# Raw edge counts turned by DMA for the last six blocks of a graph layer, instead of on TensorE

## What is computed

```python
def _L0_gnn_ref(x, edge_index, W, b):
    ...
    h = jnp.einsum('nd,od->no', x, W) + b
    deg = jnp.zeros((num_nodes,), dtype=h.dtype).at[row].add(1.0)
    deg_inv_sqrt = deg ** (-0.5)
    norm = deg_inv_sqrt[row] * deg_inv_sqrt[col]
    msg = norm[:, None] * h[col]
    out = jax.ops.segment_sum(msg, row, num_segments=num_nodes)
    return out
...
edge_index = jnp.stack([src, dst])
x = x + _L0_gnn_ref(_layernorm(x, axis=-1), edge_index, L0_gnn_W, L0_gnn_b)
x = x + _L0_ffn_ref(_layernorm(x, axis=-1)[None], ...)[0]
```

## Time and profile before

| what | value |
|---|---|
| median of three runs | 646.37 us |
| the profiled execution | 647.8 us |
| its span, first to last instruction | 646.1 us |
| TensorE busy | 550.3 us, 85% |
| VectorE busy | 477.6 us, 74% |
| ScalarE busy | 239.8 us, 37% |
| GpSimd busy | 207.8 us, 32% |
| mean granted TensorE clock | 0.94 of full speed |
| instructions | 12534 |

### The profile page before, as it was taken

How to read it: one execution, slowest core, us unless ns; L and a number is a source line. 1 busy time by engine, 2 the same in 40 slices (tenths; PEclk the granted TensorE clock), 3 DMA queues, 4 the chain that set the end, 5 groups by cost and what they waited for, 6 DMA issues and landing times.

```text
span 646.1 us, 12534 instructions
## 1 busy us (share of the span) xinstructions
PE 550.3 (85%) x3720; PEld 303.7 (47%) x3721; DVE 477.6 (74%) x1293; ACT 239.8 (37%) x366; POOL 207.8 (32%) x200
## 2 busy tenths in 40 slices
PE   1598999999989999999495999999999999999300
PEld 0243455544444455555383565656565655565100
DVE  8998966976308588898877767776767677664297
ACT  4232333233217133434542344443434343411370
POOL 2740000000000126656646344445353535141231
PEclk9989999999979999999587999999999999999755
DMA  5595111111113624434655696969696969273979
GB/s 210 192 387 213 36 34 34 34 34 34 34 34 132 259 99 144 180 136 164 209 175 156 190 292 180 290 188 286 193 274 203 282 199 265 82 127 112 242 219 277
DMA packets 51691, 110.34 MB, mean 171 GB/s; under 512 B 25618, under 2 KB 26031, under 8 KB 51632
## 3 DMA queue, kind: packets, MB, share of 16 engines
q1 hardware_dynamic: 41552, 78.06, 34.2%
q0 software_dynamic: 8896, 27.38, 20.4%
q10 hardware_dynamic: 1184, 4.20, 1.9%
HBM read 71.75 MB, written 33.67 MB: 163 GB/s over the span
## 4 chain that ended last, share of the span: by engine, by line
PE 70%; DVE 21%; issue 3%; DMA 2%; ACT 2%; DVEq 1%; POOL 0%; ACTq 0%; POOLq 0%; SPq 0%
PE ps L1883 7%; PE ps L1766 6%; PE ps L1767 6%; PE ps L1884 6%; PE ps L1885 6%; PE ps L1862 5%; PE ps L1864 5%; PE ps L1863 5%; PE ps L1690 4%; PE ps L1844 4%; PE ps L1691 3%; PE ps L1692 3%; DVE wbufs L1162 3%; DVE wbufs L1161 2%; PE ps L1634 2%
## 5 line engine op out<-in xcount | busy, mean ns | idle before, releaser
L515 POOL TENSOR_TENSOR work<-work 128x1024 f16<-128x1024 f32 x9 | 19.2, 2128 | 213.5 <-ACT work L883 213.5
L608 POOL DMA_INDIRECT acc_rows<-work,ids_out x24 | 52.3, 2180 | 106.7 <-DVE work L1487 106.7
L1766 PE MATMUL ps<-wbufs,rows_and_counts 128*128 128x512 f16 x200 | 75.8, 379 | 0.5 <-DVE wbufs L1267 0.5
L1767 PE MATMUL ps<-wbufs,rows_and_counts 128*128 128x512 f16 x200 | 75.8, 379 | 0.0
L1862 PE MATMUL ps<-rows_and_counts,wbufs 128*128 128x336 f16 (+2 forms) x256 | 74.8, 298 | 0.8 <-DVE rows_and_counts L1425 0.8
L1883 PE MATMUL ps<-wbufs,rows_and_counts 128*128 x192 | 73.8, 384 | 1.8 <-issue 1.3
L1863 PE MATMUL ps<-rows_and_counts,wbufs 128*128 128x336 f16 (+2 forms) x256 | 74.9, 298 | 0.0
L1864 PE MATMUL ps<-rows_and_counts,wbufs 128*128 128x336 f16 (+2 forms) x256 | 74.8, 298 | 0.0
L1884 PE MATMUL ps<-wbufs,rows_and_counts 128*128 x192 | 73.7, 384 | 0.0
L1885 PE MATMUL ps<-wbufs,rows_and_counts 128*128 x192 | 73.5, 383 | 0.0
L1440 DVE SCALAR_TENSOR_TENSOR wbufs<-stage,wbufs 128x1024 f16<-128x1024 f32 x56 | 67.0, 1218 | 7.4 <-ACT wbufs L910 6.9
(11 more groups left out here) (305 smaller groups left out, 1087.5 us busy)
## 6 DMA issues: line engine op xcount, KB each, us to landing
stage<-wst_in SPq DMA_DIRECT2D x72, 512.0 KB, 6.0
acc_rows<-work SPq DMA_DIRECT2D x10, 512.0 KB
x_rows<-work SPq DMA_DIRECT2D x10, 512.0 KB
t<-x_in SPq DMA_DIRECT2D x1, 4096.0 KB, 14.5
wbufs<-b_in ACTq DMA_DIRECT2D x8, 512.0 KB
wbufs<-acc_rows SPq DMA_DIRECT2D x8, 512.0 KB, 6.7
t<-x_in SPq DMA_DIRECT2D x1, 3072.0 KB, 10.2
t<-x_in SPq DMA_DIRECT2D x1, 2048.0 KB, 8.0
```

The lines of the kernel that those rows point to most:

```text
L1766: mm(o, ct_hi[:, cs], hs[:, at:at + HALF], start=(m == 0), stop=False, skip_group_check=True)
L1767: mm(o, ct_hi[:, cs], hs[:, D + at:D + at + HALF], start=False, stop=False, skip_group_check=True)
```

## The change

The raw counts of blocks 4 to 9 are turned by a transposing DMA each, from `raw16` to `ct_hi`, on SP's queue. The products of `count_turn` and the copies of `count_hi` are left out for these blocks. Two semaphores, `ct_in[0]` and `ct_in[1]`, count the transfers of even and odd blocks. ScalarE waits for the transfer of block m - 2 before it writes the first raw strip of block m into the same buffer, and TensorE waits for all six ahead of the degree products. Blocks 0 to 3 are turned as before.

```diff
+COUNTS_BY_PE = 4
...
+        ct_in = [sem(f"ct_in{i}") for i in range(2)]
...
@@ block.sync
                 sp.wait_ge(xs_done, m + 1)
                 sp.wait_ge(lin_done, m - 1)
                 sp.dma_start_transpose(xt[:, at:at + 2 * D].rearrange("p (b k) -> p b k", k=P), xs).then_inc(xt_in, 16)
+                for n, blocks in enumerate(STEP_BLOCKS):
+                    if n == m - 1 and blocks[0] >= COUNTS_BY_PE:
+                        k = blocks[0]
+                        sp.wait_ge(raw_read, 4 * k + 4)
+                        sp.dma_start_transpose(ct_hi[:, k * NP:(k + 1) * NP].rearrange("p (h d) -> p h d", d=P),
+                                               raw16[k % 2]).then_inc(ct_in[k % 2], 16)
@@ block.scalar, raw_out
                     a.activation(raw32, strip, ACT.Copy).then_inc(raw32_done, 1)
+                if j == 0 and m >= COUNTS_BY_PE + 2:
+                    act.wait_ge(ct_in[m % 2], 16 * ((m - COUNTS_BY_PE) // 2))
                 a.activation(hi, strip, ACT.Copy).then_inc(raw_read, 1)

             def count_hi(m, groups):
+                if m >= COUNTS_BY_PE:
+                    return
@@ block.tensor
             def count_turn(m, groups):
+                if m >= COUNTS_BY_PE:
+                    return
...
                     pe.wait_ge(raw_lo_done, m + 1)
-                    pe.wait_ge(count_hi_read, NG * (m + 1))
+                    pe.wait_ge(count_hi_read, NG * min(m + 1, COUNTS_BY_PE))
...
             turn(NT - 1)
-            pe.wait_ge(count_hi_read, NG * NT)
+            pe.wait_ge(count_hi_read, NG * COUNTS_BY_PE)
+            for i in range(2):
+                pe.wait_ge(ct_in[i], 16 * (NT - COUNTS_BY_PE) // 2)
```

## The result

The changed kernel took 641.11 us (median of 6 runs, 640.08 to 643.28) beside 646.06 (645.47 to 646.76) for the kernel before, a ratio of 0.9923 [0.9908, 0.9939]: 4.95 us faster where 2.99 was forecast, and 0.4 us outside the range. The profiled execution took 641.27 us (span 639.6) against 647.8 (span 646.1). The one before is 1.7 us above the median of its kernel, so the spans differ by 6.5 us where the medians differ by 4.95.

The account below looks back on a forecast made before the run. TensorE was taken to bound most steps, VectorE steps 4 and 5. Savings of 1.68 + 0.11 + 1.20 = 2.99 us from 646.37 gave 643.4 us; 8-in-10 range 641.5 to 646.0.

Parts of the forecast that it names:

- Steps 3, 6 and 7: TensorE-bound steps turning blocks 4, 7 and 8: each saves 0.45 + 0.11 us, 1.68 us together.
- Steps 4 and 5: VectorE feeds the last window: only block 6's second part, behind that window, counts, 0.11 us; the other 1.01 us become waiting.
- Block 9: In the tail: 0.44 us for its first part, 0.76 us for the second with the wait for ScalarE's copy; 1.20 us.
- the tail's clock: TensorE's clock drops to half after the degree products, slowing dense products; change counted as 0, ends 2.1 gained, 1.2 lost.
- the gap of 1.25 us behind the degree products: TensorE's idle time in the tail, at the branch for large counts; left out of the sum.
- My end for the clock: Far end of the forecast's own range: the clock's fall misses the tail's dense products, 2.1 us more gained.
- Rival 1: VectorE does not bind in steps 4 and 5, so the whole sum comes through: 4.0 us, 642.4; chance 0.08.
- Rival 2: Only the tail counts; what steps 3, 6 and 7 give is taken back: 1.2 us left, 645.2; chance 0.15.
- Rivals 3 and 4: 3: clock falls in step 5, 648.4, chance 0.08; 4: block 9's transfer lands late, from 9.1 us on, chance 0.04.

Follow-up runs that it names:

- e3: Changed kernel with TensorE's ten products for each of blocks 4 to 9 kept at their old places, read by nobody; 645.46 us, ratio 0.9985.
- e6: Changed kernel with VectorE's statistics of row blocks 2 to 9 in four pairs instead of two fours; 641.66 us, ratio 0.9925.
- e9: Kernel before with 72 unneeded one-column products at TensorE's start; 646.90 us, ratio 1.0013.
- r1: Unchanged copy of the changed kernel, measured again; 644.54 us, ratio 0.9976 to the kernel before.
- e8: Changed kernel with 50 unneeded one-column products at TensorE's start; 644.13 us, ratio 0.9963.
- r2: Unchanged copy of the changed kernel, measured again in another group; 645.82 us, ratio 0.9972 to the kernel before.
- r3: Unchanged copy of the changed kernel, measured again in another group; 644.31 us, ratio 0.9949 to the kernel before.
- e13: Kernel before with statistics in pairs and degree products spread in the linear layer, all blocks turned by TensorE, no unneeded products; 639.77 us, ratio 0.9891.
- e12b: Second measurement of the changed kernel with statistics in pairs, degree products spread and fifty unneeded products at TensorE's start; 637.40 us, ratio 0.9859.
- e8b: Changed kernel with 50 unneeded one-column products at TensorE's start, measured in another group; 643.23 us, ratio 0.9936.
- e11: Changed kernel with statistics in pairs and degree products spread in the linear layer's quarters; 641.35 us, ratio 0.9895.
- e12: Changed kernel with statistics in pairs, degree products spread and fifty unneeded products at TensorE's start; 636.81 us, ratio 0.9836.
- e10: Changed kernel with the hundred degree products spread through the third and fourth quarter of row block 8's linear layer; 644.91 us, ratio 0.9967.

## Why the prediction was right and wrong

*Steps 3, 6 and 7, 1.68 us.* Right: 0.55 + 0.55 + 0.56 = 1.66 us in the first profile, and e3, which puts the products back, has 15.21 us again.

*Steps 4 and 5, 0.11 us.* The size was right (0.13), one reason only half. Step 5 is VectorE's: the five products that took 1.36 us in the earlier trace rows took 1.72,

```profile
133.70 1.72 PE L1646 MATMUL ps<-wbufs 128*128 128x320 f16 x5
```

and e6 takes the step to 15.05. In step 4 something else gave back what the products had left. The third window and what follows, after:

```profile
117.90 0.85 PE L1646 MATMUL ps<-wbufs 128*128 128x320 f16 x5
118.86 0.44 PE L1654 MATMUL ps<-wbufs 128*128 128x320 f16 x2
119.61 0.39 PE L1704 MATMUL ps<-wbufs 128*128 128x512 f16 x1
```

and before:

```profile
118.97 0.85 PE L1634 MATMUL ps<-wbufs 128*128 128x320 f16 x5
119.66 0.43 PE L1642 MATMUL ps<-wbufs 128*128 128x320 f16 x2
120.32 0.39 PE L1690 MATMUL ps<-wbufs 128*128 128x512 f16 x1
```

From the window's start to the next weight product it is 1.71 us now and was 1.35, although the two products of the turn stood in it then. What its two further pairs wait for was not tried.

*Block 9, 1.20 us.* Right by the timelines: the linear layer runs on from its second quarter into the degree products, and e9 against r1 gives 1.21 us. The transfers took 3.4 to 4.7 us where I expected 3 to 4.5, and no wait is put down to them, at the raw copies neither; nor did the branches cost more than before in the steps.

*What failed: two terms that the sum put at nothing, the tail's clock, which I took at 0, and the gap of 1.25 us behind the degree products, which I had in the trace and left as it was.* In the first profile both went and gave 1.4 + 2.2 us; with the 2.99 that is 6.6, and the difference of the spans is 6.5. The medians show 4.95 us, so some 2 us of the 3.6; which of the other executions had the lowered clock is not recorded. The gap hangs on the place of the code (e8, e9). The change takes it away each time (four profiles of four), by having fewer products ahead of the branch and not by the turn, and in three of the four X is 3.1 to 4.5 us longer, more than the gap gave. The clock's fall isn't the change's doing: in the same kernel it is missing twice and there for 3.4 us twice (r2, r3), where the tail takes 1.4 to 1.7 us more. My end for the clock, 2.1 us down, was of the right size. The mistake was to leave the gap out of the range and to hold the stages behind as fixed: they were in the first profile, and not in r1 to r3.

*The size of the whole.* The four measurements of the changed kernel (6, 10, 12 and 6 executions) have a weighted mean ratio of 0.9960, 2.6 us, and all 34 have a median of 644.18 us, inside the range. They disagree by more than their intervals (0.9923 [0.9908, 0.9939] against 0.9972 [0.9956, 0.9988]), so one such interval is too narrow for an effect of this size. With e13 against e12b, 2.4 us, and the steps of the profile, that agrees with the sum of 2.99 to about half a microsecond. So the change's own worth was forecast nearly right, and the first measurement had some 2.4 us that came from elsewhere. Why X was 149.5 us in it and 152.6 to 154.0 us in the same code later stays open; r1 to r3 were measured on three chips, and no run here tells the chip from chance.

*The rivals.* Rival 1 (VectorE binds nowhere) fell with the 0.13 us. Rival 2 fell: steps 3, 6 and 7 kept their gain. Rivals 3 and 4 didn't come: the clock is 1.00 in step 5 and the transfer lands in 4.7 us at most, well under the 9.1 us from which on it would have been late.

## What to carry to other kernels

Read what an edit saves from the distance between starts on the bounding engine, and give it only to the steps where that engine has no wait; this held to some hundredths of a microsecond (0.56 us forecast a step, 0.55 and 0.56 measured). Before a gap marked issue or a lowered clock is put down to an edit, count the instructions ahead of it, pad the program with unneeded ones, and run the same kernel several times. Here the padding moved the median by 0.4 and 1.1 us within a group (e8 beside r1, e8b beside r3) and by some 4 us from e11 to e12, and the same changed kernel came out 1.0, 1.75, 2.7 and 4.95 us under the kernel before in four measurements. The fastest kernel (e12 and e12b, 636.8 and 637.4 us, 1.4 to 1.6% under the kernel before) came from that: the change, VectorE's statistics in pairs, the degree products spread, and fifty products at the start.

## What the runs showed of the hardware

- Fifty or seventy-two one-column products at the start of the program bring or take a gap of 1.2 to 1.7 us behind a branch over a hundred products, 180 us later. The gap is there in all six profiles with 947 or 957 products ahead of that branch and in none of the twelve with 797 to 907 or 1029; only in e13 (857) are 0.19 us of idle time shown. The time to the experts' start goes with the place as well (X 149.5 us in nine profiles of nine, against 150.8 to 154.1 in eight of nine). By what mechanism, the runs do not show.
- The clock can fall with TensorE shown busy throughout (r2, 178 to 184 us: busy 6.00 of 6.00, mean clock 0.72). What ran before was the hundred one-column products. In the fifteen profiles where they stand in one run, the clock stayed at 1.00 in the tail only three times (the first after, r1, e9). In e10 to e13, where they stand between products of 512 columns, it was 1.00 in all five profiles.
- A transposing DMA of 128x1280 in f16 within SBUF lands in 3.4 to 4.7 us, one of 128x2048 in 4.2 to 4.7, beside a busy TensorE and with no cost to it that could be seen.
